# Ten gate steps share their product with GpSimd, more first additions by DMA, and the sums of all steps dealt out anew (FP32, one core)

## The reference, cut to what matters

```python
# h: (256, 768), q: (8, 64, 768); B = 8 graphs, N = 32 nodes each, L = 64 query tokens, F = 768
hg = einsum('bnf,gf->bng', h3, Wg[:, :F])
qg = einsum('blf,gf->blg', q, Wg[:, F:]) + bg
attn = sigmoid(hg[:, :, None, :] + qg[:, None, :, :])      # (8, 32, 64, 768)
qi = einsum('bnlf,blf->bnf', attn, q)                      # product with q, sum over the 64 tokens
alpha = sigmoid(h3 @ Wq[:, :F].T + qi @ Wq[:, F:].T + bq)
hn = alpha * tanh(qi) + (1 - alpha) * h3
```

## Time and profile before

| | |
|---|---|
| median of three runs | 805.35 us (802.1 to 805.49) |
| profiled execution, its own time | 805.78 us |
| its span in the profile | 804.0 us |
| granted PE clock over the span | 0.997 |
| gate 0 (first sigmoid to end of the sums) | about 116 to 260 us |
| gate 1 | about 324 to 467 us |
| PE / DVE / POOL / ACT busy over the span | 96 / 75 / 61 / 53 % |

### The profile page before, as it was taken

The page is one execution under the profiler, slowest core; times in us unless marked ns, Lnnn a source line. Parts: engine busy times, 40 slices in busy tenths (PEclk is TensorE's granted clock), DMA queues, the critical chain, the costliest instruction groups (busy, mean ns, idle before and its releaser), DMA issues.

```text
span 804.0 us, 10573 instructions
## 1 busy us (share of the span) xinstructions
PE 770.6 (96%) x4182; PEld 640.3 (80%) x4182; DVE 599.6 (75%) x664; ACT 423.5 (53%) x508; POOL 490.8 (61%) x243
## 2 busy tenths in 40 slices
PE   7999999999999999998989999999998999998998
PEld 4668995677666799667657569999998999985897
DVE  8967139999999630999999987555986498567454
ACT  6524456777774442777867734434541454253742
POOL 0534709899998374698999936741873177805500
PEclk9999999999999999999999999999999999999999
DMA  9136427767765463385668838554463445350001
GB/s 359 45 80 235 158 79 198 171 166 209 199 182 130 167 226 118 69 220 105 142 186 201 263 125 303 183 183 164 151 220 134 157 157 202 114 236 0 2 1 40
DMA packets 28585, 126.22 MB, mean 157 GB/s; under 512 B 4084, under 2 KB 6644, under 8 KB 28152
## 3 DMA queue, kind: packets, MB, share of 16 engines
q1 hardware_dynamic: 23240, 104.24, 39.1%
q0 software_dynamic: 4176, 15.21, 10.2%
q10 hardware_dynamic: 1120, 6.10, 2.0%
HBM read 100.63 MB, written 0.79 MB: 126 GB/s over the span
## 4 chain that ended last, share of the span: by engine, by line
PE 70%; DVE 15%; POOL 5%; ACT 4%; DMA 2%; issue 2%; DVEq 0%; SPq 0%; ACTq 0%
PE ps L1156 26%; PE ps L1122 12%; DVE prod L2054 8%; PE ps L1447 6%; PE ps L1187 5%; PE ps L1494 4%; PE ps L1669 3%; ACT prod L868 2%; DVE qi_t L2076 2%; PE ps L1314 2%; PE ps L1335 2%; POOL prod L646 1%; POOL w_lo L630 1%; PE ps L1737 1%; PE ps L1315 1%
## 5 line engine op out<-in xcount | busy, mean ns | idle before, releaser
L630 POOL TENSOR_TENSOR w_lo<-w_raw,w_hi 128x1536 fp32r<-128x1536 f32 x49 | 183.2, 3749 | 145.1 <-ACT w_hi L737 145.0
L2054 DVE TENSOR_TENSOR prod<-prod,ps 128x2048 f32<-128x2048 f32 x96 | 217.4, 2282 | 2.7 <-ACT prod L868 2.4
L868 ACT ACTIVATE prod<-ps 128x1024 f32<-128x1024 f32 x192 | 185.8, 1024 | 58.2 <-PE ps L1447 56.1
L646 POOL TENSOR_TENSOR prod<-prod 128x1024 f32<-128x1024 f32 x65 | 157.3, 2424 | 37.0 <-DVE prod L2054 36.0
L737 ACT ACTIVATE w_hi<-w_raw 128x1536 fp32r<-128x1536 f32 x60 | 88.9, 1487 | 119.9 <-PE ps L1156 109.4
L1447 PE MATMUL ps<-sel_pair,h_and_q 128*128 128x512 f32 x384 | 127.7, 445 | 13.0 <-ACT prod L868 12.1
L1156 PE MATMUL ps<-w_hi,yt_hi 128*128 128x384 f32 x480 | 123.5, 338 | 3.0 <-DVE w_lo L1928 3.0
L1156 PE MATMUL ps<-w_lo,yt_hi 128*128 128x384 f32 x480 | 122.6, 336 | 0.0
L1156 PE MATMUL ps<-w_hi,yt_lo 128*128 128x384 f32 x480 | 122.6, 336 | 0.0
L1122 PE MATMUL ps<-w_raw,h_t 128*128 128x384 f32 x312 | 106.5, 486 | 0.0
L1447 PEld LDWEIGHTS ps<-sel_pair,h_and_q 128*128 128x128 f32 x384 | 66.6, 189 | 48.3 <-ACT prod L868 23.9
(11 more groups left out here) (266 smaller groups left out, 1156.3 us busy)
## 6 DMA issues: line engine op xcount, KB each, us to landing
w_raw<-weights SPq DMA_DIRECT2D x105, 768.0 KB, 4.4
prod<-prod POOLq DMA_DIRECT2D x29, 512.0 KB, 5.2
wa_in<-weights SPq DMA_DIRECT2D x6, 768.0 KB, 5.8
w_gat<-weights SPq DMA_DIRECT2D x6, 768.0 KB, 8.1
w_query<-weights SPq DMA_DIRECT2D x3, 768.0 KB, 11.9
a_vec<-gat_vectors ACTq DMA_DIRECT2D x1, 2048.0 KB, 8.6
h_and_q<-stage_hi SPq DMA_DIRECT2D x20, 96.0 KB, 2.2
h_and_q<-stage_lo SPq DMA_DIRECT2D x20, 96.0 KB, 2.2
```

Source lines behind the costliest of these rows:

```text
L630: pool.tensor_tensor(Wl[:, j, :], raw_slab(U, 0, j), Wh[:, j, :], ALU.subtract).then_inc(w_lo_by_pool, 1)
L646: pool.tensor_tensor(v[:, 0], v[:, 0], v[:, 1], ALU.add).then_inc(folded_once, 1)
L868: act.activation(slot_view(s)[:, u], args.rearrange("p b (n l) -> p (b n) l", l=LH), ACT.Sigmoid).then_inc(sigmoid_ready, 1)
L2054: TT(slot_view(s), slot_view(s), query, ALU.mult).then_inc(products_ready, 1)
```

## The change

At ten steps of each gate (BY_TWO) DVE multiplies only the lower token half, and POOL multiplies the upper one, as a new instruction ahead of the first fold of that step. POOL's product waits for the upper sigmoid only, and its first fold waits for both products. BY_DMA grows from 14 to 15 steps in gate 0 and from 15 to 20 in gate 1. The letters in KIND are dealt out anew, and with them FOLD_AT, SECOND_AT and REST_AT:

| steps of each kind (0 to 46) | gate 0 before | gate 0 now | gate 1 before | gate 1 now |
|---|---|---|---|---|
| V | 11 | 24 | 9 | 20 |
| G | 13 | 8 | 12 | 8 |
| H | 11 | 4 | 10 | 5 |
| T | 12 | 11 | 16 | 14 |
| first fold by DMA | 14 | 15 | 15 | 20 |
| product by two engines | 0 | 10 | 0 | 10 |

```diff
+BY_TWO = [(0, 5, 10, 12, 20, 24, 29, 30, 39, 42),
+          (0, 8, 12, 15, 19, 21, 23, 28, 30, 37)]
-FOLD_AT = [{8: 5, 14: 9, 17: 13, 20: 16, 22: 17, 23: 20, 26: 22, 31: 26, 35: 30, 41: 36, 44: 40, 46: 43},
+FOLD_AT = [{8: 6, 14: 9, 17: 12, 20: 16, 22: 18, 26: 21, 34: 31, 35: 30, 44: 40, 45: 42, 46: 43},
...
+        def wait_partner(eng, i, s):
+
+            if s in BY_TWO[i]:
+                eng.wait_ge(product_by_pool, (len(PARTNER[0]) if i == 1 else 0) + PARTNER[i][s])
...
+            def partner_product(i, s):
+
+                _, f, b, _ = place_of(s)
+                v = slot_view(s)[:, 1]
+                pool.wait_ge(sigmoid_ready, 2 * STEPS * i + 2 * s + 1)
+                query = qTf[:, f, b * L + LH:(b + 1) * L].unsqueeze(1).broadcast_to([P, NB, LH])
+                pool.tensor_tensor(v, v, query, ALU.mult).then_inc(product_by_pool, 1)
+
             def first_fold(i, s):
 
                 v = slot_view(s)
                 pool.wait_ge(products_ready, STEPS * i + (s + 1))
+                wait_partner(pool, i, s)
...
                 for s in range(STEPS - 1):
+                    if s in BY_TWO[i]:
+                        partner_product(i, s)
                     first_fold(i, s)
...
-                    TT(slot_view(s), slot_view(s), query, ALU.mult).then_inc(products_ready, 1)
+                    if s in BY_TWO[i]:
+                        v = slot_view(s)[:, 0]
+                        query = ps[:, 6, o:o + LH].unsqueeze(1).broadcast_to([P, NB, LH])
+                    else:
+                        v = slot_view(s)
+                        query = ps[:, 6, o:o + L].rearrange("p (u l) -> p u l", u=2).unsqueeze(2).broadcast_to([P, 2, NB, LH])
+                    TT(v, v, query, ALU.mult).then_inc(products_ready, 1)
```

More of the change, by code:

```diff
@@ L66 @@
 RAW_AT = {(u, c, j): 3 * n + j + 1 for n, (u, c) in enumerate(RAW) for j in range(3)}
[L68 to L71, removed]
-FOLD_AT = [{8: 5, 14: 9, 17: 13, 20: 16, 22: 17, 23: 20, 26: 22, 31: 26, 35: 30, 41: 36, 44: 40, 46: 43},
-           {8: 5, 11: 6, 12: 8, 13: 9, 15: 10, 16: 13, 17: 12, 20: 15, 21: 16, 22: 17, 26: 21, 31: 27, 35: 30, 38: 34, 41:
-           36, 46: 43}]
@@ L75 @@
[L75 to L80, removed]
@@ L81 @@
-REST_AT = [[(), (), (0,), (), (1,), (), (2, 3, 4), (), (), (5,), (6, 7), (), (), (8, 10), (9,), (11, 12), (), (13, 15),
[5 rows of a table removed]
+KIND = ["GGVVVVTGVTVVTGVHTVTVGTVVVVGVVVTTVHVVGVVVTHTTVGH",
+        "GHVGVVTVTTTVTTVTVVTVVGTVVVGVGTVGTGTVGVTVHVHTVHH"]
+BY_DMA = [(3, 5, 9, 11, 14, 19, 21, 24, 27, 29, 32, 35, 38, 41, 44),
+          (1, 3, 7, 11, 13, 14, 16, 18, 20, 21, 22, 24, 27, 29, 31, 34, 35, 37, 41, 44)]
+BY_TWO = [(0, 5, 10, 12, 20, 24, 29, 30, 39, 42),
+          (0, 8, 12, 15, 19, 21, 23, 28, 30, 37)]
@@ new lines @@
+FOLD_AT = [{8: 6, 14: 9, 17: 12, 20: 16, 22: 18, 26: 21, 34: 31, 35: 30, 44: 40, 45: 42, 46: 43},
+           {9: 6, 13: 8, 14: 9, 15: 10, 16: 12, 18: 13, 20: 15, 23: 18, 27: 22, 34: 29, 35: 32, 38: 34, 41: 38, 46: 43}]
+SECOND_AT = [[(0,), (1,), (), (), (), (), (), (7,), (), (), (), (), (), (13,), (), (15,), (), (), (), (), (20,), (), (), (),
+             (), (), (26,), (), (), (), (), (), (), (33,), (), (), (36,), (), (), (), (), (), (), (41,), (), (45,), (46,)],
+             [(0,), (), (), (1,), (), (3,), (), (), (), (), (), (), (), (), (), (), (), (), (), (), (), (), (), (21,), (),
+             (), (26,), (), (28,), (), (), (), (), (33,), (31,), (), (36,), (), (), (), (40,), (), (42,), (), (), (45,),
+             (46,)]]
@@ L89, in numbered @@
+REST_AT = [[(), (), (), (), (0, 2), (1,), (4,), (3,), (), (5,), (7, 8), (6,), (10,), (), (9,), (11,), (), (12, 13), (14, 15),
[5 rows of a table added]
 def numbered(keys):
     return {s: n + 1 for n, s in enumerate(keys)}
+PARTNER = [numbered(BY_TWO[i]) for i in range(2)]
 FIRST_BY_POOL = [numbered(s for s in range(STEPS - 1) if s not in BY_DMA[i]) for i in range(2)]
@@ L343, in build @@
         dma_folded = [sem(f"dma_folded{k}") for k in range(PSLOTS)]
+        product_by_pool = sem("product_by_pool")
         folded_once = sem("folded_once")
@@ L2052, in gate_product @@
                     o = (f % 2) * 256 + bb * L
-                    query = ps[:, 6, o:o + L].rearrange("p (u l) -> p u l", u=2).unsqueeze(2).broadcast_to([P, 2, NB, LH])
-                    TT(slot_view(s), slot_view(s), query, ALU.mult).then_inc(products_ready, 1)
+                    if s in BY_TWO[i]:
[5 more added lines that the diff above has]
+                    TT(v, v, query, ALU.mult).then_inc(products_ready, 1)
                 def reduce(s):
```

## The result

The changed kernel takes 808.32 us (median of 10 runs, 805.09 to 810.23) and the kernel before, run beside it, 801.43 (10 runs, 799.72 to 805.49): ratio 1.0073, interval 1.0049 to 1.0096. So it is slower by 0.7%, where the prediction had 802.4 us and 806.8 as the upper end of its range.

What follows compares the result with a forecast made beforehand. PE to ACT and DVE were taken as two side-by-side chains, PE pacing early and DVE from step 28 in gate 0; 805.78 - 0.9 - 2.2 = 802.7, median 802.25, taken as 802.4 us, range 799.6 to 806.8.

Steps and rivals of the forecast that it cites:

- Base: Whole kernel: the sum started from the profiled execution, 805.78 us, 0.4 over the median of 805.35.
- Prices: Both gates, cost per instruction: DVE's half product 1.13 us, saving 1.06; POOL's product 2.4, between 2.34 and 3.35.
- Gate 0: -0.9: Gate 0: product 47 starts at 252.4 instead of 253.2, a gain given as 0.9 us.
- Sums by DMA come late: Rival, both gates: five DMA sums landing at 9.3 us hold PE's folds or DVE's reduce; 815, at half 809; chance 0.09.
- the walk: Both gates, step-by-step reckoning of PE, DVE and POOL, with DMA sums landing at 5.2 us; 802.7 for the profiled execution.
- Its own sign: PE ahead of a fold: waits of 2 us each for POOL or a DMA would mean a forecast wrong to the slow side.
- From step 28 DVE sets the pace: Gate 0, products 28 to 47: PE is well ahead, so DVE's 54.7 us of work and 0.2 of waits decide.
- Gate 1: -2.2: Gate 1: product 47 starts at 457.9 instead of 460.1, a gain of 2.2 us, 1.4 of it a DMA wait.
- the sentence on the shared port: Both gates: VectorE instructions with two SBUF inputs contend with POOL; POOL's product beside a gate product costs nothing extra.
- PE keeps the pace throughout: Rival, both gates: gate 0 gains only 0.4 us and gate 1 about 1.0, giving 804.0; chance 0.16.
- DVE's whole saving arrives: Rival, both gates: DVE runs from the start, -5.5 us in all, giving 799.9; chance 0.14.
- POOL's product at the upper bound: Rival, both gates: POOL's product takes 3.35 us instead of 2.4, +9.5 per gate, giving 811; chance 0.06.

Runs made afterwards that it cites:

- both mends: Changed kernel with the norm's shift as an operation of one SBUF tensor and without the DMA sums of gate 0's steps 9 and 21: 803.18 us, ratio 1.0018.
- the norm mended: Changed kernel with the norm's shift (128x1) as a tensor_scalar, one tensor input in SBUF instead of two: 804.93 us, ratio 1.0043.
- gate 1 alone: Kernel before with the changed tables in gate 1 only and the norm's shift with one SBUF tensor input: 801.87 us, ratio 1.0000.

## Why the prediction was wrong

**Base.** The sum starts from 805.78, the time of an execution in which DVE had waited 3.2 us for POOL behind the gates. The next profile of the same kernel, where the weights landed earlier, does not have that wait. The kernel before is at 801.4 to 802. With the same gains the forecast would have been 798.3 to 799. The row was in the trace: a product of 4.96 us among eleven others of its line at 1.75 to 4.21. This moves the base, not the gain: the gain was forecast at 3 us and a loss of 7 was measured.

**Prices.** Half product 1.21 of duration, right. POOL's product at 2.4 was 2.58 at the mean in gate 0, inside the bounds of the earlier trace rows; 20 of them make some 4 us. With both mends PE waited for POOL 1.1 us in gate 0, between products 28 and 35, and 0.8 in gate 1. DVE's work: -1.4 forecast in gate 0 and -1.2 measured, -2.7 forecast in gate 1 and -2.1 measured with the norm mended. A small slip of the sum: by its own terms (253.2 - 252.4) gate 0 gains 0.8 and not 0.9, which changes nothing.

**"Gate 0: -0.9"**, measured +5.6. Three steps of it failed.
- "Sums by DMA come late" was bounded by 9.3 us, with five places. The landing was 11.8 and at a sixth place, step 9, which the walk took at the median of 5.2. Steps 9 to 15 took 20.3 us, 16.6 with both mends: 3.8 us, about 1 of it by the fallen clock, of which the prediction has no term. Its own sign came true: it called a wait of 2 us at PE ahead of a fold the mark of a forecast wrong to the slow side, and the waits have one of 2.2.
- The spread of the queries was not in the sum. I asked where each DMA lands, and not which other queue issues at that moment. 22 to 28 took 18.5 us, 16.6 with both mends: 2.0.
- "From step 28 DVE sets the pace" counted DVE's work from 28 to 47 as one sum, 54.7, and got 54.9. Measured with both mends: 56.7, of which DVE worked 54.9. The work was right to 0.2, but it is no less than the kernel before has there (21.1 + 33.5 = 54.7): the gain was to come from fewer waits alone. There were more, 1.8 us, 1.3 of them between 28 and 35, for PE's folds (behind POOL's addition) and a sum by DMA. In the changed kernel itself, with the two stalls ahead, 28 to 47 took 55.5 us: part of this third loss shows only once they are mended.

Against the forecast of 134.6 the gate took 6.5 us more; the three make 3.8 + 2.0 + 0.6. What held is the first half of the walk: with both mends product 28 comes 0.4 us earlier, as forecast.

**"Gate 1: -2.2"**, measured +2.0. The step that failed is the sentence on the shared port. It was used in one direction, to say that POOL's product costs nothing extra, and the norm's operations, which do have two SBUF inputs, were not looked at. That was 3.1 us by the rows (3.69 against 0.63) and 2.9 by the gate. With it mended gate 1 gained 0.9 against 133.6: up to product 24 DVE's work fell by 1.8 us, but it stood idle 1.5 more, for a copy of ACT's that waits for PE (1.2) and for PE's folds (0.8, 0.3 before); behind it the stretch shrank by 0.7, where 1.7 was forecast: DVE's work was 66.8, as forecast (66.7), and its waits 1.0 in place of 0.2.

**Rivals.** "Sums by DMA come late" is the nearest in kind. It was priced at about 6.5 to 13 us over five places and given 0.09; one late landing at a place outside its list was enough for 3.8 us. It was right in kind, and the norm's wait is in no rival. "PE keeps the pace throughout" had -0.4 and about -1.0: with both mends the gates are +1.0 and -0.9, so it describes gate 1 and the first half of gate 0, and not what follows product 28. "DVE's whole saving arrives" and "POOL's product at the upper bound" are out.

**What stays open.** The stages behind gate 1 ended at 339.1 to 340.2 us after its last product in the profiles of the kernel before and its variants with the old tables (343.9 in the first), and at 339.8 to 342.1 with the changed table in gate 1. In gate 1 alone against the kernel before, two weight subtractions on DVE (`w_lo<-w_raw,w_hi`, both inputs in SBUF) took 2.67 and 2.98 us instead of 1.98 and 2.00, which is 1.7 of the 2.1 us. All four began while POOL ran a subtraction of its own and ended 1.6 us after it: the same wait as the norm's shift. Why POOL's stood later, and took 5.0 us instead of 4.5, was not settled. The longer end takes back what gate 1 alone gained.

## What to carry to other kernels

Reckon a saving stretch by stretch, with what bounds each stretch: here DVE saved 1.6 us where PE held it, and got 0.8 more to do where it was itself the bound. Before a transfer is moved, look at which other issues and transfers stand at that time, and give it the longest landing seen in such company; before POOL gets more to do, list DVE's operations with two SBUF inputs, however small. And profile the base twice: one odd row, 3.2 us longer than in the next profile, was worth more than the gain that was forecast.
